# Rotary half-swap: two ScalarE instructions in place of two transfers, in an attention and expert block

## The reference

```python
q = (h @ wq + bq)            # per head: 1024 x 128
def _rotate_half(x):
    x1, x2 = jnp.split(x, 2, axis=-1)
    return jnp.concatenate((-x2, x1), axis=-1)
q = q * cos + _rotate_half(q) * sin
k = k * cos + _rotate_half(k) * sin
scores = jnp.einsum('bhqd,bhkd->bhqk', q, k) / math.sqrt(HD)
```

## Time and profile before

| | |
|---|---|
| median of three runs | 1116.54 us (1117.46, 1116.27, 1116.54) |
| span of the profiled execution, first to last instruction | 1115.4 us |
| PE busy | 1105.2 us, 99% |
| weight loads of PE | 1006.7 us, 90% |
| DVE busy | 834.9 us, 75% |
| ACT busy | 748.3 us, 67% |
| POOL busy | 638.1 us, 57% |
| transfers `work<-work` | 256, 128 KB each, 2.3 us to landing |

### The profile page before, as it was taken

One profiled execution on the slowest core, in us unless ns is written; L12 is line 12 of the kernel. 1 busy time (PEld: TensorE's weight loads), 2 busy tenths in 40 slices (PEclk: granted clock), 3 DMA queues, 4 the chain that ended last, 5 costly groups with the idle time before them and its releaser, 6 DMA issues.

```text
span 1115.4 us, 20396 instructions
## 1 busy us (share of the span) xinstructions
PE 1105.2 (99%) x7100; PEld 1006.7 (90%) x7100; DVE 834.9 (75%) x1978; ACT 748.3 (67%) x1584; POOL 638.1 (57%) x516
## 2 busy tenths in 40 slices
PE   9999999999999999999999999999999999999997
PEld 8999899999999999999999999999999999988897
DVE  7776777777777777777777777777777777977776
ACT  5666867666666666666666666666666666688765
POOL 2217666555555555555555555555555556777676
PEclk9999999999999999999999999999999999999999
DMA  5002412121212121212121212121211212230102
GB/s 176 1 1 62 129 39 53 39 62 39 52 39 62 39 53 39 60 39 50 37 60 39 52 39 62 39 48 44 62 38 37 50 40 57 48 110 14 39 1 76
DMA packets 33285, 56.54 MB, mean 51 GB/s; under 512 B 5792, under 2 KB 10016, under 8 KB 33184
## 3 DMA queue, kind: packets, MB, share of 16 engines
q1 hardware_dynamic: 33040, 55.21, 19.9%
q10 hardware_dynamic: 144, 0.03, 0.0%
HBM read 17.47 MB, written 4.19 MB: 19 GB/s over the span
## 4 chain that ended last, share of the span: by engine, by line
PE 95%; POOL 2%; issue 1%; ACT 1%; DMA 1%; DVE 1%; SPq 0%; POOLq 0%; ACTq 0%; DVEq 0%
PE ps_m L458 58%; PE ps_s L458 23%; PE ps_t L608 12%; PE ps_m L505 1%; DMA work<-in_attn_w 0%; POOL acc L2341 0%; POOL qk_lo L2346 0%; PE ps_m L479 0%; POOL wqk_lo L2346 0%; PE ps_t L458 0%; POOL pT_lo L2354 0%; DMA work<-work 0%; POOL acc L2330 0%; PE ps_m L666 0%; PE ps_m L667 0%
## 5 line engine op out<-in xcount | busy, mean ns | idle before, releaser
L2296 POOL TENSOR_TENSOR work<-work,rope 128x512 f32<-128x512 f32 x128 | 165.5, 1293 | 222.8 <-DMA work<-work 222.7
L1784 DVE TENSOR_TENSOR pT_lo<-ps_t,pT_hi 128x512 fp32r<-128x512 f32 (+3 forms) x408 | 210.8, 551 | 32.7 <-ACT pT_hi L1201 30.2
L1201 ACT ACTIVATE pT_hi<-ps_t 128x512 fp32r<-128x512 f32 (+3 forms) x408 | 182.8, 489 | 65.3 <-PE ps_t L608 65.1
L1777 DVE CUSTOM_DVE_ANT_0 ps_s<-ps_s,causal 128x128 f32<-128x128 f32 (+7 forms) x272 | 203.5, 767 | 6.7 <-PE ps_s L458 4.1
L2300 POOL TENSOR_TENSOR work<-work 128x512 f32<-128x512 f32 x128 | 167.6, 1310 | 10.0
L2307 POOL TENSOR_TENSOR qk_lo<-work,qk_hi 128x512 fp32r<-128x512 f32 x128 | 163.0, 1293 | 17.8 <-ACT qk_hi L1158 17.8
L1152 ACT ACTIVATE work<-ps_m,bqk 128x512 f32<-128x512 f32 x128 | 88.8, 694 | 116.5 <-PE ps_m L458 116.4
L1817 DVE SCALAR_TENSOR_TENSOR acc<-ps_m,rinv,acc 128x256 f32<-128x256 f32 x272 | 118.6, 478 | 63.0 <-PE ps_m L458 61.7
L1194 ACT ACTIVATE prob_b<-ps_s,nmax 128x640 f32<-128x640 f32 (+3 forms) x136 | 130.3, 958 | 17.9 <-DVE nmax L1777 14.6
L458 PE MATMUL ps_s<-qk_hi 128*128 128x384 f32 (+5 forms) x384 | 140.6, 366 | 0.0
L1738 DVE SCALAR_TENSOR_TENSOR work<-ps_m,bqk,rope 128x512 f32<-128x512 f32 x128 | 95.5, 746 | 54.3 <-ACT work L1152 54.0
(11 more groups left out here) (235 smaller groups left out, 2822.7 us busy)
## 6 DMA issues: line engine op xcount, KB each, us to landing
work<-work SPq DMA_DIRECT2D x256, 128.0 KB, 2.3
wst<-in_head_qk SPq DMA_DIRECT2D x16, 256.0 KB, 2.9
acc<-in_x_tiles SPq DMA_DIRECT2D x8, 256.0 KB, 6.8
wo_st<-in_L_ffn_wo SPq DMA_DIRECT2D x16, 128.0 KB, 2.4
wst<-in_pair_v SPq DMA_DIRECT2D x8, 256.0 KB, 3.0
x_rows<-acc SPq DMA_DIRECT2D x4, 512.0 KB, 3.6
wst<-in_expert SPq DMA_DIRECT2D x8, 256.0 KB, 3.0
rope<-x_rows SPq DMA_DIRECT2D x4, 512.0 KB, 4.1
```

What stands on the lines that cost most here:

```text
L1201: act.activation(pT_hi[:, slots, cols], t_bank(u, i, j)[:, 0:size * P].rearrange("p (j q) -> p j q", q=P), ACT.Copy).then_inc(t_hi.sem, t_ ...
L1777: dve.tensor_tensor_reduce(s, s, causal[:, T - (i + 1) * P:T], -1.0, ABOVE_ALL, ALU.add, ALU.min, accum_out=nmax[:, u % 2, i:i + 1]).then_ ...
L1784: dve.tensor_tensor(pT_lo[:, slots, cols], t_bank(u, i, j)[:, 0:size * P].rearrange("p (j q) -> p j q", q=P), pT_hi[:, slots, cols].bitcas ...
L2296: pool.tensor_tensor(qs[:, x % 2, :], qs[:, x % 2, :], sin_t[:, c * CH:(c + 1) * CH], ALU.mult).then_inc(sin_done.sem, sin_done.up(u, x))
```

## The change

`add_bias` becomes two ScalarE instructions of 64 partitions each. The first reads the upper half of the bank and writes the lower half of `qs`, the second reads the lower half and writes the upper half. `qb` goes, `qs` gets its two buffers and so has four, one for each x. The two transfers of each of the 128 tiles go, and with them SP's waits between the loads of weights. ACT waits for the end of the rotation of the tile four before (`rope_done`) in place of a swap two before; DVE's `rotate` waits for both halves (`crossed`), as does POOL's `turn`.

```diff
-        qb, qs, qc = work[:, 0:2, :], work[:, 2:4, :], work[:, 4:7, :]
+        qs, qc = work[:, 0:4, :], work[:, 4:7, :]
...
-        qb_done = event("qb_done", heads4)
-        swapped = [event(f"swapped_{s}", [(u, x) for u, x in heads4 if x % 2 == s], 32) for s in range(2)]
+        crossed = event("crossed", heads4)
...
                 act.wait_ge(qk_mm.sem, qk_mm.at(u, x))
-                before = q_before(u, x, 2)
+                before = q_before(u, x, 4)
                 if before:
-                    act.wait_ge(swap_of(*before).sem, swap_of(*before).at(*before))
-                act.activation(qb[:, x % 2, :], m_bank("q", u, x), ACT.Identity,
-                               bias=bqk[:, j, head_:head_ + 1]).then_inc(qb_done.sem, qb_done.up(u, x))
+                    act.wait_ge(rope_done.sem, rope_done.at(*before))
+                half, bank = HD // 2, m_bank("q", u, x)
+                act.activation(qs[0:half, x, :], bank[half:HD], ACT.Identity,
+                               bias=bqk[half:HD, j, head_:head_ + 1])
+                act.activation(qs[half:HD, x, :], bank[0:half], ACT.Identity,
+                               bias=bqk[0:half, j, head_:head_ + 1]).then_inc(crossed.sem, crossed.up(u, x))
...
-                dve.wait_ge(qb_done.sem, qb_done.at(u, x))
+                dve.wait_ge(crossed.sem, crossed.at(u, x))
...
-                pool.wait_ge(swap_of(u, x).sem, swap_of(u, x).at(u, x))
-                pool.tensor_tensor(qs[:, x % 2, :], qs[:, x % 2, :], sin_t[:, c * CH:(c + 1) * CH],
+                pool.wait_ge(crossed.sem, crossed.at(u, x))
+                pool.tensor_tensor(qs[:, x, :], qs[:, x, :], sin_t[:, c * CH:(c + 1) * CH],
...
-            def swap(u, x):
-                sp.wait_ge(qb_done.sem, qb_done.at(u, x))
-                before = q_before(u, x, 2)
-                if before:
-                    sp.wait_ge(rope_done.sem, rope_done.at(*before))
-                half = HD // 2
-                sp.dma_start(qs[0:half, x % 2, :], qb[half:HD, x % 2, :]).then_inc(swap_of(u, x).sem, 16)
-                sp.dma_start(qs[half:HD, x % 2, :], qb[0:half, x % 2, :]).then_inc(swap_of(u, x).sem, 16)
-                swap_of(u, x).up(u, x)
```

More of the change, by code:

```diff
@@ L413, in m_bank @@
             return ps_m[:, shared[use] % 2, :]
-        def swap_of(u, x):
-            return swapped[x % 2]
         def ring3(u, x):
@@ L2299, in turn @@
                 pool.wait_ge(cos_done.sem, cos_done.at(u, x))
-                pool.tensor_tensor(qc[:, ring3(u, x), :], qc[:, ring3(u, x), :], qs[:, x % 2, :],
+                pool.tensor_tensor(qc[:, ring3(u, x), :], qc[:, ring3(u, x), :], qs[:, x, :],
                                    ALU.add).then_inc(rope_done.sem, rope_done.up(u, x))
@@ L2623, in start @@
                 load_rope()
-                swap(2, 0)
                 load_v_weights(1)
                 load_qk_weights(0, 1)
-                swap(2, 1)
                 load_o_weights(0, 1)
-                swap(2, 2)
-                swap(2, 3)
-                swap(3, 0)
                 keep_x1(0, 0)
@@ L2636, in start @@
                 keep_x1(0, 1)
-                swap(3, 1)
-                swap(3, 2)
                 keep_x1(1, 1)
-                swap(3, 3)
             def head(u):
                 n, p, r = u + 1, pair_of(u), (u - 2) % 4
-                swap(n, 0)
                 if r == 0 and p + 1 < PAIRS:
@@ L2647, in head @@
                     load_v_weights(p + 1)
-                swap(n, 1)
-                swap(n, 2)
                 if r == 2:
@@ L2652, in head @@
                     load_o_weights(p + 1, 0)
-                swap(n, 3)
                 if r == 3:
@@ L2657, in ends @@
             def ends():
-                swap(LAST - 1, 0)
                 load_expert(2, 0)
-                swap(LAST - 1, 1)
-                swap(LAST - 1, 2)
-                swap(LAST - 1, 3)
                 load_expert(2, 1)
[L2664 to L2667, removed]
                 load_expert(2, 2)
```

## The result

The changed kernel takes 1156.7 us (median of four runs, 1156.23 to 1158.11) against 1117.0 us before (here the median of four runs, 1116.27 to 1118.29): 1.036 times as long, with an interval of 1.0341 to 1.0371. That is 39.7 us lost where 25 were forecast, and outside the forecast range. The span of the profiled execution is 1154.3 us, 38.9 more than before.

The account below looks back on a forecast made before the run. PE, busy 1105.2 of 1115.4 us, was taken as the bound. A mean 0.78 us over 28 units (21.8) plus 3.1 in opening and closing made 25 on the span, 1140.4; with 1.1 for the median, 1141.5 us, range 1127 to 1150.

Parts of the forecast that it names:

- 2. outputs(u,0): PE's bank take at outputs(u,0), freed by DVE's second accumulate pair: PE has lost 0.32 us in the unit by here.
- the pair's spacing: On ACT at add_bias: halves of 0.69 us start 0.58 us apart, so the pair ends 0.58 us later than one.
- The bound above: Upper bound for a half on ACT: 0.725 us with a step of 0.62, giving 1147 us.
- Step 1: DVE's rotate(n,0) waits for ACT, low_p and the accumulate pairs come 0.40 us later; PE loses 0.26 at project_q(n,1).
- step 3: DVE's rotate(n,1), row_max and low_o come 0.84 us late; PE's loss in the unit reaches 0.56 at out_project(u,0,0).
- Step 4: DVE is busy up to rotate(n,2), still 0.84 us late; PE's loss reaches 0.79 at out_project(u,0,1).
- Step 5: ACT's exponent(u,7), 0.37 us later, delays DVE's rotate(n,3) by 0.10; PE's loss in the unit reaches 0.89 at project_v.
- The opening and closing parts: Four head units outside the 28, same steps in other orders: 0.78 us each, 3.1 us, bounds 0 and twice that.
- cheaper halves: Rival: each ACT half costs nearer 0.6 us and DVE's room eats most of it; 1127 us, chance 0.16.
- a time by partitions: Rival, faster: an ACT half takes half the time, so the pair ends as early as before; 1113 us, chance 0.04.
- no change: Rival: the room of DVE and PE hides everything; 1116.5 us, chance 0.04.
- Worse, 1154: Rival: ACT falls behind through the whole unit, losing the full 0.58 us twice per unit, 37 us in all; chance 0.06.

Follow-up runs that it names:

- pair that overlaps (0.58): Against the original: one straight 128-partition instruction, no transfers or half-swap, plus a full straight one into an unused buffer ahead in units 5 to 29; 1134.39 us (1.0154).

## Why the prediction was wrong

The mechanism was right: a half costs the whole, DVE's rotate waits for the pair, and PE loses at the bank takes that were named; nothing of the removed transfers was on PE's path in the units. The sizes were wrong, in both directions. On the span 25.0 us were forecast and 38.9 measured. The missing overlap brought 14.3 us more over 27 units (0.53 each), my working of the rest had 5.7 too many (0.57 measured for 0.78), and the opening, the closing and one more unit took 9.2 where I had 3.9 (five times 0.78): 13.9 together. What PE had lost behind each take in the unit of the forecast, in us:

| behind the take | forecast | pair that overlaps (0.58) | changed kernel |
|---|---|---|---|
| 1. project_q(n,1) | 0.26 | 0.24 | 0.37 |
| 2. outputs(u,0) | 0.32 | 0.25 | 0.38 |
| project_q(n,2) | not seen | 0.26 | 0.46 |
| 3. out_project(u,0,0) | 0.56 | 0.53 | 0.78 |
| 4. out_project(u,0,1) | 0.79 | 0.53 | 0.87 |
| scores(n,2) | not seen | 0.53 | 0.99 |
| 5. project_v | 0.89 | 0.61 | 1.21 |

(From the starts of the matmul four behind each take in the traces, and of the second at scores(n,2), laid together at the unit's start.)

- **The step that failed** is the pair's spacing: "Back to back, ACT starts the next instruction 0.58 us after an L1152 ..., so the pair ends 0.58 us later than the one did". That was read from two instructions that start on the same partition. In the changed kernel the second half starts 0.70 us after the first, and the next instruction 0.71 after that: DVE gets the pair 0.69 later, ACT's own work 0.82 later. The bound above (a step of 0.62) was too low for the same reason: both ends were taken from rows in which no instruction changes its first partition, and no such row was in the trace. Between the changed kernel and the one with two full instructions that overlap it is 0.53 us a unit, 14 us in 27.
- Step 1 and step 3: with the spacing that I assumed they come out right (0.24 for 0.26, 0.53 for 0.56), so the reading of the weight load held until 0.055 us after DVE's end and 0.11 more stood. The changed kernel's 0.37 is 0.24 and the 0.12 of spacing.
- Between them I missed a take, project_q(n,2) behind rotate(n,1). It is hidden at a spacing of 0.58 (it starts as late as the take ahead) and costs 0.08 at 0.70.
- Step 4 was read wrongly. "DVE is busy all the way to rotate(n,2)" is not so; before:

```profile
493.59 0.88 DVE L1784 TENSOR_TENSOR pT_lo<-ps_t,pT_hi 128x512 fp32r<-128x512 f32 x2
495.12 0.88 DVE L1817 SCALAR_TENSOR_TENSOR acc<-ps_m,rinv,acc 128x256 f32<-128x256 f32 x2 [0.65 <-PE ps_m L458]
```

  DVE waits there 0.65 us for PE and makes its lateness good; in the kernel with the overlapping pair nothing is lost at this take where I had 0.23. In the changed kernel 0.1 is lost all the same, by another way: ACT is by now so late that it starts add_bias(n,2) 0.95 us behind its old place in the unit (514.84 less 19.43 against 494.46), and rotate(n,2) waits for it. The near agreement of 0.79 and 0.87 is an accident.
- Step 5 was the right mechanism with the wrong size, 0.33 instead of 0.10, and in two places: PE loses 0.10 of it at scores(n,2), which waits for exponent(u,7) itself, and the rest at project_v. The pair that overlaps costs nothing at scores(n,2). exponent(u,7) starts 1.41 us after the first half (519.47 to 520.88) and not 1.16, so it is 0.62 late beside the rest in place of 0.37; less the same 0.27 of room that leaves 0.35.
- The opening and closing parts: 3.1 us forecast (3.9 with the unit outside the 27 distances), 6.4 and 2.8 measured. Some 2 to 2.6 us of it are the meeting of DVE and POOL, which I had costed at nothing in the sentence that POOL's earlier end "only widens a room that is there"; it holds for the 28 units and failed in the one place where POOL's idle time served DVE. The rest, about 7 us, goes with the pair in the units outside the 28: 2.1 of it lie between units 2 and 3 (32.17 us for 30.07), and the kernel that has its pairs in units 5 to 29 alone closes as before (206.1 us from unit 31 on, against 208.9 in the changed kernel). How it divides over the takes there was not tried.
- "No wait of PE for POOL is on its list" was misread: one stands there, 1.0 us for `prob_b`, in the opening. It is 1.0 us in the changed kernel too and plays no part.
- The rivals: cheaper halves, a time by partitions and no change all fell with 686 ns a half. "Worse, 1154" came nearest in number and named part of it, that ACT falls behind through the unit, but not the cause.

A kernel whose rotate does not wait for the pair, since it needs only the bank, wasn't tried: ACT and DVE would then read one bank at once.

## What to carry to other kernels

Before an instruction is split by partitions, look whether its parts start on the same partition as their neighbours: each change costs the overlap, 0.12 us on ACT at 512 elements, also for the instruction behind. And before an idle wait is taken out as worthless, look at what ran beside it: POOL's 1.95 us of waiting gave DVE 3.2 us, and the wait that PE got in its place can bring a lower clock behind it. A list of the places where an engine late by x makes PE wait should be checked for the places where it catches up, too.

## What the runs showed of the hardware that was not expected

- ACT holds an instruction until the one ahead has ended when its input or its output starts on another partition (0 and 64 here) than in the instruction ahead; 12 to 25 ns lie between end and start in place of an overlap of 0.09 to 0.15 us. The number of partitions plays no part, and neither does the crossing itself.
- 64 partitions cost ACT as much as 128: 682 to 686 ns against 694 at 512 elements. At 256 elements it is 457 to 469 ns, where an exponent on 128 partitions takes 477.
- DVE's scaling of 128x256 in SBUF, 0.40 us alone, takes up to 1.45 us beside POOL's instructions, four of them 4.6 to 4.7 us instead of 1.38. POOL's instructions beside it keep their 1.28 to 1.3 us.
- After a wait of PE of 1.8 us, TensorE's granted clock fell from 1.00 to 0.50 for 3.4 us in one profiled execution and stayed at 1.00 in another with the same wait; the fall cost 1.6 us.
